# Row-tiled bound scores: one head in each 64-row half of the array, issued in twos, with both heads' scores in one block

## The reference, cut to what matters

```python
attn = jax.nn.softmax(jnp.einsum('bhsd,bhtd->bhst', q, k), axis=-1)
ctx = jnp.einsum('bhst,bhtd->bhsd', attn, v)
```

## Time and profile before

| what | value |
|---|---|
| median of 3 runs | 526.01 us (525.68 to 526.38) |
| profiled execution, span from first to last instruction | 526.2 us |
| instructions | 8110 |
| TensorE matmuls busy | 470.9 us |
| VectorE / ScalarE / GpSimd busy | 407.4 / 356.4 / 183.4 us |
| HBM | 14.31 MB read, 6.42 MB written |

### The profile page before, as it was taken

The page is one execution under the profiler, slowest core; times in us unless marked ns, Lnnn a source line. Parts: engine busy times, 40 slices in busy tenths (PEclk is TensorE's granted clock), DMA queues, the critical chain, the costliest instruction groups (busy, mean ns, idle before and its releaser), DMA issues.

```text
span 526.2 us, 8110 instructions
## 1 busy us (share of the span) xinstructions
PE 470.9 (89%) x2358; PEld 160.8 (31%) x2358; DVE 407.4 (77%) x668; ACT 356.4 (68%) x452; POOL 183.4 (35%) x214
## 2 busy tenths in 40 slices
PE   5339379999999999999999999999999999999992
PEld 3115123232233332222333322223333223232252
DVE  3578989999888868998887689998876899981022
ACT  3865212578968756789788567887775678878851
POOL 9556900331534221315432303153323031634200
PEclk9859769999999999999999999999999999999996
DMA  6001326110111110101101001111010111010205
GB/s 211 0 1 56 121 75 208 30 25 12 48 32 27 33 25 10 46 24 33 36 20 38 19 15 41 27 30 43 14 45 11 22 37 12 1 13 1 87 7 159
DMA packets 49289, 22.25 MB, mean 42 GB/s; under 512 B 36532, under 2 KB 40756, under 8 KB 49268
## 3 DMA queue, kind: packets, MB, share of 16 engines
q1 hardware_dynamic: 48736, 21.83, 15.3%
q10 hardware_dynamic: 532, 0.16, 0.3%
HBM read 14.31 MB, written 6.42 MB: 39 GB/s over the span
## 4 chain that ended last, share of the span: by engine, by line
PE 69%; DVE 16%; ACT 5%; issue 5%; DMA 3%; POOL 1%; SPq 1%; DVEq 0%; POOLq 0%; ACTq 0%
PE banks L1091 19%; PE banks L1176 19%; PE banks L1166 17%; DVE neg_half L986 6%; PE banks L1159 3%; ACT probs L804 3%; PE banks L1155 3%; DVE run L945 2%; DVE probs L917 1%; PE banks L1112 1%; PE banks L1100 1%; DMA x_sb<-in_x_dram 1%; DVE parts L921 1%; DVE parts L919 1%; DVE parts L915 1%
## 5 line engine op out<-in xcount | busy, mean ns | idle before, releaser
L986 DVE TENSOR_REDUCE neg_half<-banks 128x1 f32<-128x512 f32 x512 | 323.7, 685 | 46.1 <-PE banks L1091 44.3
L804 ACT ACTIVATE probs<-banks 128x1024 f32<-128x1024 f32 x256 | 247.5, 1021 | 74.4 <-PE banks L1166 73.6
L1091 PE MATMUL banks<-k_op,q_op 96*128 96x512 bf16 x512 | 181.2, 384 | 19.7 <-DVE V L937 11.4
L1166 PE MATMUL banks<-q_op,k_op 99*128 99x512 bf16 x512 | 151.5, 379 | 1.2 <-DMA q_op<-max_parts 0.6
L1176 PE MATMUL banks<-probs,v_op 128*32 128x512 f32 x1024 | 136.4, 605 | 0.4 <-ACT probs L804 0.4
L1091 PEld LDWEIGHTS banks<-k_op,q_op 96*128 96x128 bf16 x512 | 43.6, 97 | 170.0 <-DVE neg_half L986 126.3
L1166 PEld LDWEIGHTS banks<-q_op,k_op 99*128 99x128 bf16 x512 | 49.0, 98 | 65.3 <-issue 11.9
L1176 PEld LDWEIGHTS banks<-probs,v_op 128*32 128x32 f32 x1024 | 20.1, 108 | 53.5 <-issue 52.3
L643 POOL TENSOR_TENSOR qk_f<-qk_f 128x512 f32<-128x512 f32 x12 | 12.5, 1039 | 52.6 <-ACT qk_f L789 52.6
L968 DVE TENSOR_TENSOR rec<-banks,parts 128x512 f32<-128x512 f32 x4 | 2.8, 692 | 34.6 <-PE banks L1155 34.6
L564 POOL TENSOR_TENSOR max_parts<-max_rows,zero_rows 16x128 bf16<-16x128 f32 x16 | 7.1, 444 | 56.7 <-DVE max_rows L982 56.3
(11 more groups left out here) (163 smaller groups left out, 456.0 us busy)
## 6 DMA issues: line engine op xcount, KB each, us to landing
q_op<-q_dram SPq DMA_DIRECT2D x32, 144.0 KB
k_op<-k_dram SPq DMA_DIRECT2D x32, 144.0 KB
k_dram<-parts SPq DMA_DIRECT2D x10, 256.0 KB, 3.9
parts<-ctx_dram SPq DMA_DIRECT2D x8, 256.0 KB, 4.2
mat_sb<-in_mats_dram SPq DMA_DIRECT2D x2, 768.0 KB, 7.7
q_dram<-parts SPq DMA_DIRECT2D x6, 256.0 KB, 3.2
ctx_dram<-ctx_sb SPq DMA_DIRECT2D x64, 18.0 KB
x_sb<-in_x_dram SPq DMA_DIRECT2D x4, 256.0 KB, 5.6
```

The lines of the kernel that those rows point to most:

```text
L804: a.activation(probs[:, (2 * step + e) % 4, :, :], banks[:, 2 * e:2 * e + 2, :], ACT.Exp).then_inc(b_read, 1)
L986: v.tensor_reduce(neg_half[:, s, u:u + 1], src, axis=AX.X, op=ALU.max, negate=True).then_inc(a_read, 1)
L1091: mm(dst, q_op[0:MAX_ROW, s, e, P * c:P * c + P], k_op[0:MAX_ROW, s, e, CHUNK * h:CHUNK * h + CHUNK], start=True, stop=True).then_inc(a_re ...
L1166: last = mm(bank(2 * e + h), k_op[0:MAX_ROW + PARTS, s, e, P * step:P * step + P], q_op[0:MAX_ROW + PARTS, s, e, CHUNK * h:CHUNK * h + CHU ...
```

## The change

A now contracts over 64 rows instead of 96: eight of the nine part products. Head 0 keeps its data in rows 0 to 71 (A uses 0 to 63, the ninth product is in 64 to 71) and its maxima in 96 to 98. Head 1 has its data in rows 64 to 127 and the ninth product in rows 0 to 7, its maxima in rows 32 to 34, so that its B spans all 128 rows. The As of both heads lie in the two 64-row halves of the array. place_of orders them by twos: head 0 and head 1 of the same block. The places are handed out in units of two; unit 0 also has T. A step is two As (and T in one of eight), B of both heads, two As, values, and the product if there is one. LEAD is 13 places. To get the eight products into 64 rows, the slots of k in DRAM begin with another part (slot + 1). load_pair has two transfers for head 0 and six for head 1; place_max has one for each part and head.

```diff
@@ -14,11 +14,13 @@
 KEY_TILES = T // P
 PARTS = 3
 ROWS = PARTS * PARTS * HD
-MAX_ROW = 96
+MAX_ROWS = (96, 32)
 
 
 PROJECT_EARLY, PROJECT_FROM, PROJECT_GAP = 4, 2, 5
-LEAD = 12
+LEAD = 13
+UNITS = 16
+LEAD_UNITS = 6
 SPLIT_STEP = 5
 A_PLACES = 33
 PV_BANK, A_BANK = 4, 5
@@ -300,6 +302,15 @@
 
             return [divmod(n, A_PLACES) for n in range(first, last)]
 
+        def unit_places(unit):
+
+            return (2 * unit, 2 * unit + 1) if unit == 0 else (2 * unit + 1, 2 * unit + 2)
+
+        def place_of(k):
+
+            u = k if k < 2 else k - 1
+            return u % 2, u // 4, u // 2 % 2
+
         def exists(it, pair, k):
 
 
@@ -322,11 +333,18 @@
 
         turns, place_turns = [], []
         for t in range(SETS * KEY_TILES):
-            at = A_PLACES + LEAD
-            here = places(at + A_PLACES * t // KEY_TILES, at + A_PLACES * (t + 1) // KEY_TILES)
-            place_turns.append(range(len(turns), len(turns) + len(here)))
-            turns += here
+            here = []
+            for half in range(2):
+                ahead, unit = divmod(LEAD_UNITS + 2 * (t % KEY_TILES) + half, UNITS)
+                pair = t // KEY_TILES + 1 + ahead
+                here.append([(pair, k) for k in unit_places(unit)])
+                if unit == 0:
+                    here[-1].append((pair, 2))
+            place_turns.append((range(len(turns), len(turns) + len(here[0])),
+                                range(len(turns) + len(here[0]), len(turns) + len(here[0]) + len(here[1]))))
+            turns += here[0] + here[1]
             turns += [name for name, step in PRODUCT_STEP.items() if step == t]
+        assert turns[0] == divmod(A_PLACES + LEAD, A_PLACES)
         assert (len(turns) + 1) % 3 == 0
 
         def product_bank(name):
@@ -382,20 +400,38 @@
             def load_pair(p, s):
 
 
-                for e in range(2):
-                    sp.dma_start(q_op[0:ROWS, s, e, :],
-                                 bass.AP(q_dram.tensor, (p * 2 + e) * (PARTS * HD * T),
-                                         [[0, PARTS], [T, PARTS * HD], [1, T]])).then_inc(op_in[s][e], 16)
-                    sp.dma_start(k_op[0:ROWS, s, e, :],
-                                 bass.AP(k_dram.tensor, (p * 2 + e) * (SLOTS * HD * T),
-                                         [[HD * T, PARTS], [T, PARTS * HD], [1, T]])).then_inc(op_in[s][e], 16)
+                q0, k0 = p * 2 * (PARTS * HD * T), p * 2 * (SLOTS * HD * T)
+                sp.dma_start(q_op[0:ROWS, s, 0, :],
+                             bass.AP(q_dram.tensor, q0, [[0, PARTS], [T, PARTS * HD], [1, T]])
+                             ).then_inc(op_in[s][0], 16)
+                sp.dma_start(k_op[0:ROWS, s, 0, :],
+                             bass.AP(k_dram.tensor, k0, [[HD * T, PARTS], [T, PARTS * HD], [1, T]])
+                             ).then_inc(op_in[s][0], 16)
+
+                q1, k1 = q0 + PARTS * HD * T, k0 + SLOTS * HD * T
+                sp.dma_start(q_op[64:112, s, 1, :],
+                             bass.AP(q_dram.tensor, q1, [[0, 2], [T, PARTS * HD], [1, T]])
+                             ).then_inc(op_in[s][1], 16)
+                sp.dma_start(k_op[64:112, s, 1, :],
+                             bass.AP(k_dram.tensor, k1, [[HD * T, 2], [T, PARTS * HD], [1, T]])
+                             ).then_inc(op_in[s][1], 16)
+                sp.dma_start(q_op[112:128, s, 1, :],
+                             bass.AP(q_dram.tensor, q1, [[T, 2 * HD], [1, T]])).then_inc(op_in[s][1], 16)
+                sp.dma_start(k_op[112:128, s, 1, :],
+                             bass.AP(k_dram.tensor, k1 + 2 * HD * T, [[T, 2 * HD], [1, T]])).then_inc(op_in[s][1], 16)
+                sp.dma_start(q_op[0:HD, s, 1, :],
+                             bass.AP(q_dram.tensor, q1 + 2 * HD * T, [[T, HD], [1, T]])).then_inc(op_in[s][1], 16)
+                sp.dma_start(k_op[0:HD, s, 1, :],
+                             bass.AP(k_dram.tensor, k1 + 4 * HD * T, [[T, HD], [1, T]])).then_inc(op_in[s][1], 16)
 
             def place_max(p, s):
 
                 sp.wait_ge(max_parts_ready, p + 1)
                 for i in range(PARTS):
-                    sp.dma_start(q_op[MAX_ROW + i:MAX_ROW + i + 1, s, :, :],
-                                 max_parts[:, s % 2, i, :]).then_inc(max_in[s % 2], 16)
+                    for e in range(2):
+                        sp.dma_start(q_op[MAX_ROWS[e] + i:MAX_ROWS[e] + i + 1, s, e, :],
+                                     max_parts[KEY_TILES * e:KEY_TILES * (e + 1), s % 2, i, :]
+                                     ).then_inc(max_in[s % 2], 16)
 
             def stage_v(p, s):
 
@@ -422,7 +458,7 @@
 
                 for slot in range(SLOTS if t else PARTS):
                     sp.dma_start((k_dram if t else q_dram)[b * HEADS:(b + 1) * HEADS, slot, :, :],
-                                 parts[:, t, slot % PARTS, 2 * b:2 * b + 2, :].rearrange("p n t -> p (n t)")
+                                 parts[:, t, (slot + 1) % PARTS if t else slot, 2 * b:2 * b + 2, :].rearrange("p n t -> p (n t)")
                                  ).then_inc(parts_out[b], 16)
 
             sp.wait_ge(q_split, 2)
@@ -511,7 +547,9 @@
             g.memset(q_op[:, :, :, :], 0.0).then_inc(cleared, 1)
             pool.wait_ge(cleared, 1)
             pool.wait_ge(keys_cleared, 1)
-            g.memset(k_op[MAX_ROW:MAX_ROW + PARTS, :, :, :], 1.0).then_inc(ones_set, 1)
+            for e in range(2):
+                ones = g.memset(k_op[MAX_ROWS[e]:MAX_ROWS[e] + PARTS, :, e, :], 1.0)
+            ones.then_inc(ones_set, 1)
             pool.wait_ge(ones_set, 1)
             g.memset(v_op[:, :, :, :, :], 0.0).then_inc(v_set, 1)
             pool.wait_ge(v_set, 1)
@@ -981,11 +1019,12 @@
                     dve.wait_ge(a_ready, n + 1)
                     v.tensor_copy(max_rows[:, (s + 1) % 2, :], src[0:2 * KEY_TILES, 0:P]).then_inc(a_read, 1)
                     return
-                u = k if k < 2 else k - 1
+                e, c, h = place_of(k)
+                u = 16 * e + 2 * c + h
                 dve.wait_ge(a_ready, n + 1)
                 v.tensor_reduce(neg_half[:, s, u:u + 1], src, axis=AX.X, op=ALU.max, negate=True
                 ).then_inc(a_read, 1)
-                if u == 31:
+                if k == A_PLACES - 1:
                     dve.wait_ge(a_read, n + 1)
                     v.tensor_reduce(neg_max[:, s, :], neg_half[:, s, :].rearrange("p (c h) -> p c h", h=2),
                                     axis=AX.X, op=ALU.min).then_inc(half_combined, 1)
@@ -994,7 +1033,7 @@
                 read_place(0, pair, k, bank(A_BANK + a_count(0, pair, k) % 3))
 
             def one_step(t, it):
-                for turn in place_turns[t]:
+                for turn in (*place_turns[t][0], *place_turns[t][1]):
                     read_place(it, *turns[turn], turn_bank(turn))
                 branch(t, it)
 
@@ -1084,12 +1123,11 @@
                     nc.tensor.transpose(dst[0:2 * KEY_TILES, 0:P], neg_max[:, (pair + 1) % 2, :],
                                         ident[:, :]).then_inc(a_ready, 1)
                     return
-                u = k if k < 2 else k - 1
-                e, c, h = u // 16, u // 2 % 8, u % 2
-                if u % 16 == 0:
-                    pe.wait_ge(op_in[s][e], (it + pair // SETS + 1) * 32)
-                mm(dst, q_op[0:MAX_ROW, s, e, P * c:P * c + P],
-                   k_op[0:MAX_ROW, s, e, CHUNK * h:CHUNK * h + CHUNK],
+                e, c, h = place_of(k)
+                if k < 2:
+                    pe.wait_ge(op_in[s][e], (it + pair // SETS + 1) * (96 if e else 32))
+                mm(dst, q_op[64 * e:64 * e + 64, s, e, P * c:P * c + P],
+                   k_op[64 * e:64 * e + 64, s, e, CHUNK * h:CHUNK * h + CHUNK],
                    start=True, stop=True).then_inc(a_ready, 1)
 
             def project(m, now):
@@ -1162,9 +1200,10 @@
 
                 if not (first(p) and step == 0):
                     pe.wait_ge(b_read, p * 16 + 2 * step + e - 1)
+                used = P if e else MAX_ROWS[0] + PARTS
                 for h in range(2):
-                    last = mm(bank(2 * e + h), k_op[0:MAX_ROW + PARTS, s, e, P * step:P * step + P],
-                              q_op[0:MAX_ROW + PARTS, s, e, CHUNK * h:CHUNK * h + CHUNK], start=True, stop=True)
+                    last = mm(bank(2 * e + h), k_op[0:used, s, e, P * step:P * step + P],
+                              q_op[0:used, s, e, CHUNK * h:CHUNK * h + CHUNK], start=True, stop=True)
                 last.then_inc(b_ready, 1)
 
             def values(p, s, step):
@@ -1181,13 +1220,14 @@
 
                 t = j * KEY_TILES + step
                 todo = place_turns[t]
-                fill_turn(it, todo[0])
+                for turn in todo[0]:
+                    fill_turn(it, turn)
                 if step == 0:
-                    pe.wait_ge(max_in[j % 2], (it * 2 + j // 2 + 1) * 16 * PARTS)
```

(7 more changed lines are left out.)

## The result

| | before | after |
|---|---|---|
| median | 526.19 us (4 runs, 525.68 to 529.74) | **543.67 us** (4 runs, 541.26 to 547.33) |
| profiled execution, span | 526.2 us | 545.6 us |
| first load of q to first B | 37.33 us (60.50 to 97.83) | 43.63 us (62.65 to 106.28) |
| first B to last B (the loop) | 406.95 us (97.83 to 504.78) | 418.28 us (106.28 to 524.56) |

What follows compares the result with a forecast made beforehand. TensorE was taken as the bound, with little room behind it. Per-pair changes of -1.1, +0.4, -1.4 and -0.7 us over the passes gave -9.8, with +0.5 before the loop -9.3: from 526 to 517 us, range 507 to 534.

Steps and rivals of the forecast that it cites:

- items 1 and 2: Array, per plain step: A matmuls in twos -0.43 us, +0.03; two more shape changes +0.24; from 2.84 to 2.65.
- The drain: Rival: each of the two extra tile-shape changes on TensorE costs 0.26 us, a step 2.97; 538 us, chance 0.12.
- the halves that take turns: Rival: the array's halves don't run abreast, a step takes 3.08 us; 540 us, chance 0.08.
- my upper bound: TensorE's extra shape changes: each waits for the running matmul's tail and an uncovered weight load, 0.26 us each.
- item 5: SP's queue: extra loads per pair hidden; six maxima transfers for three, new ones at 0.33 us each, +0.4 us.
- The third rival: Rival: maxima transfers on SP cost 0.63 us each and the queue becomes the bound; 531 us, chance 0.12.
- third pair: Third pair of a pass: TensorE with eight steps, three products and stalls takes 24.9 us, -1.4.
- fourth pair: Fourth pair of a pass: 29.1 us, -0.7, with 0.9 for VectorE's two operations before the first A bank is freed.
- item 6: Before the loop: 12 more loads on SP and one more place, +0.5 us, bounds 0 and +3.
- First and second pair: Per pass: first pair 23.3 us, -1.1; second pair, held by the chain through the maxima, 24.15 us, +0.4.
- The landing that I found at 249.9: Second pair: the third maxima transfer lands at 249.9, B starts at 250.09; read as a chain without TensorE time.

## Why the prediction was wrong

The two stretches of the profiled executions grew by 17.6 us, forecast was -9.3: a miss of 27. It comes apart like this, by the pairs of the profiled executions.

**Right: the array (items 1 and 2).** A step was forecast at 2.65 and is 2.61; the As of a slot start together; B follows after 0.32 us; the stall of the earlier trace rows ahead of a first pair's B is gone. The drain and the halves that take turns, the two rivals at 538 and 540, are excluded: no step is near their 2.97 and 3.08 us, and with two transfers the loop is shorter than before. The rule of the Trainium skill, that a switch of the tiling mode drains the array (page TensorEngine Tiling (Array Packing), section Key Properties), may describe what happens, but here the switch costs some 0.10 us (0.32 for 0.22 from A to B) and not the 0.26 of my upper bound.

**The step that failed (item 5, the maxima on SP).** I priced a maxima transfer of 8 rows at 0.33 us, arguing from a store of 9 rows at 0.43, though the row of the very same operation stood at 0.63. It is 0.69. The 0.33 came from taking register work off the store's time, and no run shows such a term. The third rival, which takes the row as it is, was the right one, and its mark, over 0.5 per transfer, is met. It had the second pair at +1.9, and +1.9 it is (25.68 for 23.75). Over the loop, five pairs end in such a wait (the second of each pass, and the last but one of the 16); against the kernel with two transfers they lose 10.6 us, where the forecast had 1.6. On top of it comes what neither the forecast nor the rival had: the granted clock falls after three of the four waits at the start of a third pair, and such a pair takes 1.6 us more (27.44 and 27.47, against 25.89 at full clock), together 4.8. That, the way in (5.8 over what both had) and the fourth pair (2.1) make up the 12 to 13 us between the rival's 531 and the measured 544.

**The second step that failed (item 6, before the loop).** Forecast +0.5 with an upper bound of 3, measured +6.3. I counted SP's issues and one more place. What was not counted: the order of twos makes the *second* A need head 1, whose loads land last (2.3 us of wait); the clock then rises 3.7 us later, counted from the first load; products that stood among 128-row As now stand among 64-row As; and the first maxima have six transfers too (B waits 0.81 us for them). With 24-row pieces 3.4 us come back. The rest, 2.3 us over the kernel before, was not taken apart by an experiment.

**A term of the sum misread (third pair).** I put three products into it. The earlier trace rows show eight matmuls more than in a plain pair (138 for 130), which is four products. With those, and 1.06 us per product as measured for my 0.96, 8 x 2.61 + 4 x 1.06 + 0.8 is 25.9: the 25.85 measured with two transfers. The gain is 0.5 and not 1.4, over the loop 3.1 us less.

**A stall seen and not priced in full (fourth pair).** The item named VectorE's two operations ahead of the first A bank and gave 29.1; measured 29.8, no gain at all. Moving one of the two away gives 28.94. The mechanism was right, the size off by 0.7, 2.1 us over three pairs.

**First and second pair without the maxima.** With two transfers the first gains 0.83 for a forecast of 1.1, and in the loop's first pass, where it took only 23.53 us before, 0.12: 1.8 us over the loop. For the second I said "no TensorE time stands in this chain: no gain". The kernel before with one transfer shows that the chain was not what bound it, and with two transfers the new order gains 0.36 there, and 1.14 in the first pass, whose second pair before ended in a wait of 0.62: 2.3 us over the loop. The landing that I found at 249.9 ahead of a B at 250.09 was a coincidence, and no wait stood in that row.

**The loop's first pair.** It takes 26.10, as against 23.41 in the kernel with two transfers. Five other kernels with the new order, two of them with two transfers, show 26.05 to 26.07, with the clock at 0.50 for some 7 us there, and the other three lose 0.6 to 1.4 us more; so the 2.7 us are the clock and not the maxima. Why one execution keeps the clock is open. It is hardly the kernel: its mean granted clock is 0.952 to 0.961 over ten runs, and the profiled one is the fastest of them, with 0.961. Its loop of 400.25 us is thus a good case, and 402.9, as with pieces of 24, nearer the usual one.

Sum of the misses: 5.8 (way in), 9.0 (waits), 4.8 + 2.7 (clock), 3.1 (third pair), 2.1 (fourth), 1.8 (first), less 2.3 (second): 27.0. The terms of the loop are taken against the kernel with two transfers, whose first pair had the better clock; that they add up follows from taking them so.

The chances were wrong in the same place. A rival that rests on a measured row (0.12) stood against a forecast that rests on an estimate below that row (0.57); the nearest row should have carried the forecast, and the estimate the rival.

## What to carry to other kernels

Price a small transfer with the row of the same kind of transfer, here by the count and not by the bytes, and ask of each one whether it stands between a result and its first use: four loads more per pair, needed much later, cost nothing; three maxima transfers more per pair, with a matmul waiting, cost 21 us of the loop of the kernel before, and four more cost 18 in the new one (15 without the first pair's clock). If such transfers can't be fewer, issue each as soon as its piece is ready. When an order by twos asks for two operands where the old one asked for one, look at the first use of the second operand as well as at the steady state, and add to an idle time of TensorE what the clock may cost after it, here 1.6 us for a wait of 2.2. A landing just ahead of a start is a bound only if the row of the start shows a wait.
